# Seven half products for eight in the q, k, gate and v projections of a linear-attention layer

## The chip, the cores and the metric

The kernel runs on one core of a Trainium2 chip. The metric is the device time in microseconds (us) of one execution. TensorE is called PE in the rows of the profile, its weight loads PEld, VectorE DVE, ScalarE ACT, GpSimd POOL, and SyncE SP, whose queue issues transfers.

## The reference

The layer takes 1024 tokens (4 batches of 256) of 512 features. 32 heads of 128 make q, k and v (silu of a projection) and a gate (sigmoid of a projection); a decayed causal attention without softmax, an RMS norm over all heads, the gate and an output projection follow. Then a residual, a layer norm and a small mixture of low-rank experts on a base matrix.

```
qkv = silu(x @ qkv_w.T)                       # 1024 x 512 by 512 x 12288
q, k, v = heads of qkv                        # 32 heads of 128
attn = scan over blocks of 32 tokens: (q k^T * decay) v + (q * decay) kv
xf = attn * rsqrt(mean(attn^2) + eps) * norm_w
x1 = layernorm(x + (sigmoid(x @ gate_w.T) * xf) @ out_w.T)
...
out = layernorm(x1 + x1 @ base_W.T + base_b + routed low-rank experts of x1)
```

## The kernel before

**Numbers.** Every large product is computed in three passes: each operand is split in a high part (a copy to the type fp32r, on ScalarE) and a low part (what is left, a subtraction on VectorE), and TensorE adds high x high, high x low and low x high into one PSUM bank (`mm3`, L736 to L738). So every weight chunk, q, k, v, the masked scores and the gated attention cost one ScalarE copy and one VectorE subtraction (`minus`, L425) beside the matmuls.

**Stages.** The heads run in 8 groups of 4. In a group each head s has a q, a k and a gate projection: 4 slices of 128 features by two halves of 512 tokens, so 2 x 4 x 3 matmuls of 512 columns each for q, k and gate. The values of the four heads come together (8 token tiles x 4 x 3 matmuls of 512 columns). `scores` and `attention` use matmuls of 256 and 128 columns, four batches in a row. The output projection of the group before (8 tiles x 4 heads x 3 matmuls) lies at the head s = 1 of the next group. After the last group come the last output products, the sum of squares, the first layer norm, transposes, router, base product and second layer norm: about the last 70 us.

**Order.** Nothing is scheduled by a tool. Each engine runs its own list in the order of the code and waits on counters (semaphores). PSUM has 8 banks: 0 to 3 are filled in turn by projections, 4 to 7 hold scores, attention and output. A projection may start when the bank that it takes has been read (`bank_free`), that is four projections earlier; each projection bank is read once, by one silu or tanh.

**Loads.** Weights come as 170 chunks of 256 KB into 5 buffers (`raw`) and are split into 10 buffers (`wh`, `wl`). GpSimd does nothing in the groups; it works in the last 70 us, where it adds the residual (L701), the bias (L707) and the statistics of the layer norms (L691 to L694). The squares for the RMS norm are added by VectorE (L481).

## Time and profile before

| | us |
|---|---|
| median of 3 runs | 1094.51 (1093.79 to 1096.12) |
| profiled execution, its own time | 1093.89 |
| its span on the core | 1092.1 |
| PE busy | 1077.2 (99%), 5403 matmuls |
| DVE busy | 664.7 (61%) |
| ACT busy | 533.3 (49%) |
| POOL busy | 47.5 (4%) |

1.8 us of the profiled execution's own time lie outside its span. A matmul's recorded duration is longer than the distance to the next one, because matmuls are pipelined; the distance between starts is what a matmul costs.

### The profile page before, as it was taken

The page shows a single profiled execution, that of the slowest core. Times are in us where ns is not written, and L with a number is a line of the kernel's source. Part 1 is how long each engine was busy: PE and PEld are TensorE (multiplying, and loading weights), DVE is VectorE, ACT ScalarE, POOL GpSimd, SP SyncE. Part 2 cuts the span into 40 slices and gives each one's busy share as a digit, 9 for nine tenths or more (in the row PEclk, how much of TensorE's full clock was granted, in tenths as well). Part 3 has the DMA queues.
Part 4 walks back from the last instruction along what each step waited for, and adds up shares of the span by engine and source line. Part 5 has one row for each costly group of instructions (what it writes and reads, how often), then busy time and mean ns, then how long its engine had stood idle before and what let it go on. Part 6 is the DMA issues. An engine that isn't in the chain of part 4 may idle for free.

```text
span 1092.1 us, 14420 instructions
## 1 busy us (share of the span) xinstructions
PE 1077.2 (99%) x5403; PEld 914.6 (84%) x5403; DVE 664.7 (61%) x1308; ACT 533.3 (49%) x987; POOL 47.5 (4%) x89
## 2 busy tenths in 40 slices
PE   9999999999999999999999999999999999999996
PEld 7888888888888888888888888888888888888784
DVE  6477653774547635676437755486456674477766
ACT  7465541555416543465416555165433654265433
POOL 1000000000000000000000000000000000000365
PEclk9999999999999999999999999999999999999998
DMA  7031111111102102111011111021020110211202
GB/s 258 18 117 34 54 32 41 54 40 49 53 21 79 42 20 73 52 36 53 18 55 54 35 53 54 20 60 62 20 73 33 55 53 5 68 54 34 73 1 78
DMA packets 34055, 56.95 MB, mean 52 GB/s; under 512 B 4416, under 2 KB 8896, under 8 KB 33984
## 3 DMA queue, kind: packets, MB, share of 16 engines
q1 hardware_dynamic: 29088, 51.55, 14.5%
q10 hardware_dynamic: 4896, 4.46, 1.4%
q8 instruction: 43, 0.70, 0.3%
q14 instruction: 28, 0.23, 0.1%
HBM read 53.90 MB, written 2.10 MB: 51 GB/s over the span
## 4 chain that ended last, share of the span: by engine, by line
PE 96%; POOL 1%; DVE 1%; DMA 0%; issue 0%; ACT 0%; SPq 0%; POOLq 0%
PE ps L736 31%; PE ps L738 30%; PE ps L737 30%; PE ps L828 1%; PE ps L807 1%; PE ps L809 1%; PE ps L830 1%; POOL acc L701 0%; DMA acc<-xt 0%; POOL rstd L693 0%; POOL neg_mean L691 0%; PE ps L889 0%; ACT acc L367 0%; POOL var_eps L692 0%; PE ps L899 0%
## 5 line engine op out<-in xcount | busy, mean ns | idle before, releaser
L736 PE MATMUL ps<-xh,wh 128*128 128x512 f32 x764 | 302.4, 396 | 0.0
L738 PE MATMUL ps<-xh,wl 128*128 128x512 f32 x764 | 298.4, 391 | 0.0
L737 PE MATMUL ps<-xl,wh 128*128 128x512 f32 x764 | 297.7, 390 | 0.0
L266 ACT ACTIVATE sig<-ps 128x512 f32<-128x512 f32 x192 | 110.3, 592 | 148.9 <-PE ps L738 133.4
L738 PEld LDWEIGHTS ps<-xh,wl 128*128 128x128 f32 x764 | 143.4, 188 | 31.5
L736 PEld LDWEIGHTS ps<-xh,wh 128*128 128x128 f32 x764 | 143.7, 188 | 28.7 <-DVE wl L425 0.3
L737 PEld LDWEIGHTS ps<-xl,wh 128*128 128x128 f32 x764 | 143.8, 188 | 28.3
L284 ACT ACTIVATE s<-sfull 128x384 fp32r<-128x384 f32 x128 | 67.2, 525 | 117.8 <-DVE sfull L449 117.8
L736 PE MATMUL ps<-wh,xh 128*128 128x512 f32 x288 | 114.0, 396 | 0.3 <-DVE xl L425 0.3
L738 PE MATMUL ps<-wh,xl 128*128 128x512 f32 x288 | 113.0, 392 | 0.0
L737 PE MATMUL ps<-wl,xh 128*128 128x512 f32 x288 | 112.8, 392 | 0.0
L425 DVE TENSOR_TENSOR wl<-raw,wh 128x512 fp32r<-128x512 f32 x170 | 106.9, 687 | 4.0 <-ACT wh L345 3.0
L425 DVE TENSOR_TENSOR vl<-sig,vh 128x512 fp32r<-128x512 f32 x64 | 43.6, 691 | 100.3 <-ACT vh L272 100.3
L736 PE MATMUL ps<-wh,yh 128*128 128x512 f32 x256 | 100.0, 391 | 0.0
L738 PE MATMUL ps<-wh,yl 128*128 128x512 f32 x256 | 99.7, 389 | 0.0
L737 PE MATMUL ps<-wl,yh 128*128 128x512 f32 x256 | 99.7, 389 | 0.0
L292 ACT ACTIVATE sfull<-ps 128x256 f32<-128x256 f32 x64 | 23.4, 380 | 155.4 <-PE ps L830 155.4
L492 DVE TENSOR_TENSOR acc<-acc,ps 128x512 f32<-128x512 f32 x56 | 38.5, 688 | 92.8 <-PE ps L738 92.8
L443 DVE TENSOR_TENSOR sfull<-ps,dec 128x256 f32<-128x256 f32 x128 | 53.7, 420 | 58.7 <-PE ps L809 58.7
L257 ACT ACTIVATE wh<-raw 128x512 fp32r<-128x512 f32 x160 | 88.7, 620 | 1.6 <-DMA raw<-stream 1.6
L425 DVE TENSOR_TENSOR q<-sig,q 128x512 fp32r<-128x512 f32 x64 | 44.3, 693 | 61.7 <-ACT q L272 61.7
L425 DVE TENSOR_TENSOR s<-sfull,s 128x384 fp32r<-128x384 f32 x128 | 71.0, 555 | 7.8
(123 smaller groups left out, 1659.4 us busy)
## 6 DMA issues: line engine op xcount, KB each, us to landing
raw<-stream SPq DMA_DIRECT2D x170, 256.0 KB, 2.9
dec<-decay ACTq DMA_DIRECT2D x34, 128.0 KB, 2.0
acc<-xt SPq DMA_DIRECT2D x8, 256.0 KB, 4.8
raw<-x SPq DMA_DIRECT2D x8, 256.0 KB, 2.6
out<-acc SPq DMA_DIRECT2D x8, 256.0 KB, 2.0
ar<-lora_router SPq DMA_DIRECT2D x1, 288.0 KB, 3.1
sq<-base_b SPq DMA_DIRECT2D x1, 256.0 KB, 3.1
ident<-ident_in SPq DMA_DIRECT2D x1, 64.0 KB, 2.7
```

What stands on the lines that cost most here:

```text
L257: nc.scalar.activation(wh[:, u % AHEAD, :], raw[:, (AHEAD + u) % RAW, :], ACT.Copy)\
L266: nc.scalar.activation(sig[:, n % 2, :], ps[:, PROJ_B + i % 4, :], ACT.Silu).then_inc(silu_full, 1)
L284: nc.scalar.activation(sh[:, b, :], sfull[:, b % 2, 0:SC], ACT.Copy).then_inc(s_hi, 1)
L292: nc.scalar.activation(by_batch(sfull[:, e, 0:SEQ]), att_banks(e, SEQ, SC), ACT.Copy)\
L425: return nc.vector.tensor_tensor(dst, full, f32(hi), ALU.subtract)
L443: nc.vector.tensor_tensor(full[:, SEQ:W].rearrange("p (a n) -> p a n", a=2), part[:, SEQ:W].rearrange("p (a n) -> p a n", a=2), dec[:, s % ...
L492: nc.vector.tensor_tensor(acc[:, t, :], acc[:, t, :], ps[:, AO_B + t % 2, :], ALU.add)\
L736: nc.tensor.matmul(dst, wt[0], mv_[0], start=start, stop=False)
L737: nc.tensor.matmul(dst, wt[0], mv_[1], start=False, stop=False)
L738: return nc.tensor.matmul(dst, wt[1], mv_[0], start=False, stop=stop)
L807: nc.tensor.matmul(ps[:, S_B + b, SEQ:W], kh[:, q0 + P:q0 + SEQ], q2[:, :, q0 + P:q0 + SEQ], start=True, stop=False)
L809: nc.tensor.matmul(ps[:, S_B + b, SEQ:SC], kl[:, q0 + P:q0 + SEQ], qh[:, q0 + P:q0 + SEQ], start=False, stop=True).then_inc(s_done, 1)
```

## The change

The operands of the projections are cut in 2 x 2 halves: features of x in two halves, tokens in two halves, weight columns in two blocks. The product of such matrices is made of 7 half products in place of 8 (Strassen's method in Winograd's form). A block of work is one such product: the two columns blocks are q and k of one head (`qk0` to `qk3`), the gates of two heads (`g01`, `g23`), or two pairs of heads for the values (`V0`, `V1`, by token tiles). A group has the eight blocks QK0, V0, V1, G01, QK1, G23, QK2, QK3.

- The seven token operands (four quarters and three sums) are made once, at the start, on VectorE and GpSimd. Their high and low parts take 7 x 1024 columns each (before 4 x 1024).
- The seven weight operands of a block are four loaded units of 256 columns and three sums, which GpSimd makes in three additions (`sums`). ScalarE copies the high parts in two instructions of 768 and 1024 columns, VectorE subtracts twice.
- Half product p1 goes to bank 0. ScalarE copies bank 0 to bank 1 (`u2_copy`); p6 adds onto bank 1, p2 onto bank 0. ScalarE copies bank 1 to bank 2 (`u3_copy`); p7 adds onto bank 2, p3 onto bank 1. p5 has bank 3 and is copied to SBUF (`p5_copy`). VectorE adds it to bank 2 (`c22_add`) and to bank 1 (`c12_add`). p4 adds onto bank 2 and is issued in the next block, behind its p1. Bank 0, 2 and the two sums are the four results.
- A half product is 6 matmuls of 512 columns for q, k and gates, and 12 of 256 columns for the values.
- The high parts of q and k come from a second silu in place of a copy; the value's split and the splits of y are made per head and per tile, in wider or rearranged instructions.
- `scores` and `attention` are issued in two parts of two batches each.
- The squares are added by GpSimd (`add_squares`), and the next attention part on ScalarE waits for that addition, since both use the buffer `sq`. The head weights `norm_w` are applied to the output weights in place of y.
- The output projection stands behind V1 and uses banks 0 and 3. Loads are blocks of 512 KB into two stage buffers; decay tables are issued by SP in place of ScalarE.

```diff
+UNIT = {1: 0, 5: 1, 6: 2, 2: 3, 7: 4, 3: 5, 4: 6}
...
-            def project(g, i, c, e, ready=None):
-
-                bank_free(g, i)
-                r = c % AHEAD
-                for k in range(KT):
...
-                    last = mm3(ps[:, PROJ_B + i % 4, :], (wh[:, r, tile(k)], wl[:, r, tile(k)]),
-                               (xh[:, k, half(e)], xl[:, k, half(e)]), k == 0, k == KT - 1)
...
+            def features(i, bank, name, start, stop):
+
+                slot = (SLOT[name] + UNIT[i]) % RING
+                for k in range(2):
+                    last = mm3_onto(ps[:, bank, :], (wh[:, slot, tile(k)], wl[:, slot, tile(k)]),
+                                    (xh[:, i - 1, half(k)], xl[:, i - 1, half(k)]), start and k == 0, stop and k == 1)
...
+            def values(i, bank, step, start, stop):
+
+                for t in range(2):
+                    dst = ps[:, bank, t * U:t * U + U]
+                    tok = 2 * step + t
+                    for k, name in enumerate(("va", "vb")):
...
+                        last = mm3_onto(dst, (xh[:, i - 1, xs], xl[:, i - 1, xs]), (wh[:, slot, :], wl[:, slot, :]),
...
+            def p1(n):
...
+                pe.wait_ge(c11_out, n)
...
+            def p4(n):
...
+                pe.wait_ge(c22_added, n + 1)
+                product(4, B2, n, stop=True)
...
+            def with_scores(n, h):
+                p1(n)
+                p4(n - 1)
+                p5(n)
+                scores(h, 0)
+                p6(n)
+                scores(h, 1)
+                p2(n)
+                p7(n)
+                p3(n)
...
+            def sums(g, name):
...
+                nc.gpsimd.tensor_tensor(stage[:, s, 1:5:3, :], stage[:, s, 0:6:5, :],
+                                        stage[:, s, 7:8, :].broadcast_to([P, 2, U]), ALU.add).then_inc(t_part, 1)
...
+                nc.gpsimd.tensor_tensor(stage[:, s, 2, :], stage[:, s, 1, :], stage[:, s, 5, :], ALU.add)\
...
+                nc.gpsimd.tensor_tensor(stage[:, s, 6, :], stage[:, s, 2, :], stage[:, s, 3, :], ALU.add)\
...
+            def u3_copy(n):
+                act.wait_ge(p_done[6], n + 1)
+                act.wait_ge(c21_out, n)
+                act.wait_ge(c22_added, n)
+                copy(ps[:, B2, :], ps[:, B1, :]).then_inc(cp12, 1)
...
+            def part(h, e):
+                act.wait_ge(att_done, 2 * h + e + 1)
+                act.wait_ge(sq_added, 2 * h + e)
+                copy(by_batch(sq[:, 0:SEQ]), att_banks(e, SEQ, SC)).then_inc(att_part, 1)
...
+            def c22_add(n):
+                dve.wait_ge(p_done[7], n + 1)
...
+                nc.vector.tensor_tensor(c22_pre, ps[:, B2, :], p5s, ALU.add).then_inc(c22_added, 1)
```

**VectorE, around one head's scores.** Before, in the middle of a group (`sfull` is the masked score, `s` its split, `wl` a weight's low part, `q` and `kl` low parts of q and k):

```order
L443 TENSOR_TENSOR sfull<-ps,dec 128x256 [waits s_done,s_lo]
L446 TENSOR_TENSOR sfull<-ps,dec 128x256
L449 TENSOR_TENSOR sfull<-sfull 128x128 [waits s_parts]
L425 TENSOR_TENSOR s<-sfull,s 128x384 [waits s_hi] x2
L425 TENSOR_TENSOR wl<-raw,wh 128x512 [waits split_hi] x5
L425 TENSOR_TENSOR q<-sig,q 128x512 [waits silu_hi] x2
L425 TENSOR_TENSOR kl<-sig,kh 128x512 [waits silu_hi] x2
```

After, in block G23 (`stg` holds the two sums; L852 is `c22_add`, L859 `c12_add`):

```order
L819 TENSOR_TENSOR q<-stg,q 128x512 [waits c21_out,q1_full]
L819 TENSOR_TENSOR wl<-stage,wh 128x768 [waits t_hi]
L892 TENSOR_TENSOR sfull<-ps,dec 128x2x256 [waits dec_in1,sc_done,s_lo]
L894 TENSOR_TENSOR sfull<-ps,dec 128x2x256
L898 TENSOR_TENSOR sfull<-sfull 128x2x128 [waits s_parts]
L819 TENSOR_TENSOR s<-sfull,s 128x768 [waits s_hi]
L892 TENSOR_TENSOR sfull<-ps,dec 128x2x256 [waits sc_done,s_lo]
L894 TENSOR_TENSOR sfull<-ps,dec 128x2x256
L898 TENSOR_TENSOR sfull<-sfull 128x2x128 [waits s_parts]
L819 TENSOR_TENSOR wl<-stage,wh 128x1024 [waits t_hi]
L852 TENSOR_TENSOR stg<-ps,stg 128x512 [waits c22_out,k1_lo,cp5,p7_done]
L859 TENSOR_TENSOR stg<-ps,stg 128x512 [waits c12_out,k0_lo,cp5,p3_done]
```

The addition for which p4 of TensorE waits (L852) now stands behind both masks of the head and a weight's low part.

**ScalarE, from one head's q and k to the next copies.** Before:

```order
L266 ACTIVATE sig<-ps 128x512 [waits silu_lo,proj_done] x2
L272 ACTIVATE q<-sig 128x512 [waits silu_full]
L266 ACTIVATE sig<-ps 128x512 [waits silu_lo,proj_done]
L272 ACTIVATE q<-sig 128x512 [waits silu_full]
L266 ACTIVATE sig<-ps 128x512 [waits silu_lo,proj_done]
L272 ACTIVATE kh<-sig 128x512 [waits silu_full] x2
```

After, from the end of block QK1 into G23 (L394 is a silu, L350 a copy; the last row but one is `p5_copy`):

```order
L394 ACTIVATE kh<-stg 128x512 [waits sc_done,c22_added]
L394 ACTIVATE stg<-stg 128x512 [waits k1_hi]
L394 ACTIVATE kh<-stg 128x512 [waits sc_done,c12_added]
L394 ACTIVATE stg<-stg 128x512 [waits k0_hi]
L350 ACTIVATE vh<-v 128x1024 [waits att_done]
L350 ACTIVATE ps<-ps 128x512 [waits c12_added,p1_done]
L394 ACTIVATE stg<-ps 128x512 [waits q0_lo,p4_done]
L394 ACTIVATE q<-ps 128x512 [waits sc_done]
L350 ACTIVATE stg<-ps 128x512 [waits c22_added,c12_added,p5_done]
L350 ACTIVATE wh<-stage 128x768 [waits p4_done,t_sum]
```

The copy from bank 0 to bank 1 (`ps<-ps`) now stands behind the four silus of k and the copy of the values, and what TensorE, VectorE and ScalarE do in a block depends on each other in both directions.

## Rows read from the trace of the kernel before

**Rows 1.** The page: busy time, granted clock by slices, chain of waits.

```profile
PE 1077.2 (99%) x5403; PEld 914.6 (84%) x5403; DVE 664.7 (61%) x1308; ACT 533.3 (49%) x987; POOL 47.5 (4%) x89
...
PEclk9999999999999999999999999999999999999998
...
PE 96%; POOL 1%; DVE 1%; DMA 0%; issue 0%; ACT 0%; SPq 0%; POOLq 0%
```

**Rows 2.** TensorE in order of time (start, us, engine, line, operation), at 299 to 317 us.

```profile
299.74 0.39 PE L736 MATMUL ps<-wh,yh 128*128 128x512 f32 x1
...
314.47 0.39 PE L738 MATMUL ps<-wh,yl 128*128 128x512 f32 x1
314.70 0.28 PE L736 MATMUL ps<-s,vh 128*128 128x256 f32 x1
314.81 0.28 PE L737 MATMUL ps<-s,vh 128*128 128x256 f32 x1
314.93 0.28 PE L738 MATMUL ps<-s,vl 128*128 128x256 f32 x1
...
317.00 0.46 PE L736 MATMUL ps<-xh,wh 128*128 128x512 f32 x1
317.29 0.40 PE L737 MATMUL ps<-xl,wh 128*128 128x512 f32 x1
```

**Rows 3.** Groups of ScalarE and VectorE (count, busy us, mean ns, idle before).

```profile
L266 ACT ACTIVATE sig<-ps 128x512 f32<-128x512 f32 x192 | 110.3, 592 | 148.9 <-PE ps L738 133.4 <-DVE q L425 14.7 <-DVE vl L425 0.8
...
L284 ACT ACTIVATE s<-sfull 128x384 fp32r<-128x384 f32 x128 | 67.2, 525 | 117.8 <-DVE sfull L449 117.8
...
L425 DVE TENSOR_TENSOR wl<-raw,wh 128x512 fp32r<-128x512 f32 x170 | 106.9, 687 | 4.0 <-ACT wh L345 3.0 <-ACT wh L257 1.0
L425 DVE TENSOR_TENSOR s<-sfull,s 128x384 fp32r<-128x384 f32 x128 | 71.0, 555 | 7.8
L443 DVE TENSOR_TENSOR sfull<-ps,dec 128x256 f32<-128x256 f32 x128 | 53.7, 420 | 58.7 <-PE ps L809 58.7
```

**Rows 4.** A projection's last matmul and the ScalarE instruction that reads it.

```profile
343.47 0.39 PE L738 MATMUL ps<-xh,wl 128*128 128x512 f32 x1
...
343.90 0.60 ACT L279 ACTIVATE gate<-ps 128x512 f32<-128x512 f32 x1 [1.12 <-PE ps L738]
```

**Rows 5.** GpSimd's groups, then VectorE and GpSimd in the last 70 us.

```profile
L701 POOL TENSOR_TENSOR acc<-acc,raw 128x512 f32<-128x512 f32 x5 | 6.4, 1283 | 0.8 <-ACT acc L362 0.8
...
L694 POOL TENSOR_TENSOR shift<-neg_mean,rstd 128x1 f32<-128x1 f32 x16 | 3.4, 212 | 1.3
```

**Rows 6.** VectorE and GpSimd in order of time, where both work.

```profile
1030.54 0.73 DVE L565 SCALAR_TENSOR_TENSOR acc<-acc,rms,raw 128x512 f32<-128x512 f32 x1
...
1030.78 0.55 POOL L694 TENSOR_TENSOR shift<-neg_mean,rstd 128x1 f32<-128x1 f32 x1
...
1036.72 0.69 DVE L425 TENSOR_TENSOR xl<-ps,xh 128x512 fp32r<-128x512 f32 x1 [0.61 <-ACT xh L372]
1036.76 1.29 POOL L701 TENSOR_TENSOR acc<-acc,raw 128x512 f32<-128x512 f32 x1
...
1058.33 0.22 DVE L603 TENSOR_TENSOR equal<-prob,top 128x60 f32<-128x60 f32 x1
...
1067.17 5.01 POOL L727 TENSOR_TENSOR acc<-acc,raw 128x512 f32<-128x512 f32 x4 [10.06 <-ACT raw L386]
...
1067.35 1.19 DVE L603 TENSOR_TENSOR equal<-prob,top 128x60 f32<-128x60 f32 x1
```

**Rows 7.** The start: token chunks reaching ScalarE, TensorE's third projection.

```profile
5.53 0.63 ACT L350 ACTIVATE xh<-acc 128x512 fp32r<-128x512 f32 x1 [0.90 <-DMA acc<-xt]
6.51 0.63 ACT L350 ACTIVATE xh<-acc 128x512 fp32r<-128x512 f32 x1 [0.35 <-DMA acc<-xt]
...
12.42 0.50 PE L736 MATMUL ps<-xh,wh 128*128 128x512 f32 x1
```

**Rows 8.** The page: weight loads, issue to landing.

```profile
raw<-stream SPq DMA_DIRECT2D x170, 256.0 KB, 2.9
```

More of the change, by code:

```diff
@@ L23 @@
 W = 512
+U = 256
 SC = SEQ + P
@@ new lines, in after_gates, with qk1 @@
+            def after_gates(n, h, first, second):
+                u2_copy(n)
+                g21_out(n - 1)
+                first()
+                p5_copy(n)
+                part(h, 0)
+                square(h, 0)
+                u3_copy(n)
+                part(h, 1)
+                square(h, 1)
+                q0_out(n, h + 1)
+                second()
+                k1_out(n, h + 1)
+                k0_out(n, h + 1)
+                values_hi(h + 1)
+            def qk1(g):
+                after_gates(NB * g + QK1, HG * g, lambda: sums_hi(g, "g23", "A"), lambda: sums_hi(g, "g23", "B"))
@@ new lines, in _, with product, units_ready @@
+            NAMES = {QK0: "qk0", G01: "g01", QK1: "qk1", G23: "g23", QK2: "qk2", QK3: "qk3"}
+            def product(i, bank, n, start=False, stop=False):
+                b = n % NB
+                if b in (V0, V1):
+                    last = values(i, bank, b - V0, start, stop)
+                else:
+                    last = features(i, bank, NAMES[b], start, stop)
+                last.then_inc(p_done[i], 1)
+            def units_ready(n, part):
+                b = n % NB
+                name = "vb" if b in (V0, V1) else NAMES[b]
+                pe.wait_ge(t_lo, 2 * load_no(n // NB, name) + (1 if part == "A" else 2))
@@ L870, in _ @@
[L870 to L875 removed]
+                    last = nc.tensor.matmul(ps[:, S_B + b, SEQ:SC], kl[:, q0 + P:q0 + SEQ], qh[:, q0 + P:q0 + SEQ],
+                                            start=False, stop=True)
+                last.then_inc(sc_done, 1)
@@ new lines, in _ @@
+            pe.wait_ge(zeros_set, 1)
+            zero = s2[:, 0, :, :].rearrange("p b n -> p (b n)")
+            for i in range(WARMUP):
+                nc.tensor.matmul(ps[:, B1 + i % 2, :], zero[:, 0:P], zero[:, 0:W], start=True, stop=True,
+                                 skip_group_check=True)
+            for g in range(GROUPS):
+                n, h = NB * g, HG * g
+                qk0(g)
+                v0(g)
+                v1(g)
+                if g > 0:
+                    output(g)
+                g01(g)
+                with_attention(n + QK1, h)
+                with_scores(n + G23, h + 1)
+                with_attention(n + QK2, h + 1)
+                with_scores(n + QK3, h + 2)
```

1554 lines of the change are left out of this document (1101 added, 453 removed).

## The prediction

> **What bounds the kernel now.** I read the page first: PE is busy for 99% of the span at full granted clock (the slices show 9 in all but the last), and the chain of waits is 96% PE [rows 1]. The kernel is bound by the number of matmul columns. Then TensorE in order of time, for what a matmul costs: from 299.74 to 314.47 us lie 65 starts of 512-column matmuls, 14.73 / 65 = 0.2266 us each. 256-column matmuls start 0.11 to 0.12 us apart; I take 0.118. The section of four batches takes 317.00 - 314.70 = 2.30 us, and the matmul behind it is late by 0.06 (0.29 where 0.2266 is usual), together about 0.1 us for entering and leaving a section of short matmuls [rows 2]. The other engines have room: ACT 49%, DVE 61%, POOL 4% [rows 1]. ScalarE's silu waited 133 us in total for TensorE, and VectorE's masks 59 us [rows 3]: they wait for PE, hardly ever PE for them.
>
> **What TensorE saves.** q, k and gates had 32 x 3 x 2 x 4 x 3 = 2304 matmuls of 512 columns; 7/8 of them is 2016. 288 x 0.2266 = 65.3 us less. The values had 768 matmuls of 512 columns (174.0 us) and get 8 x 2 x 84 = 1344 of 256 columns (1344 x 0.118 = 158.6 us): 15.5 us less. Scores and attention go in 128 parts of two batches in place of 64 of four: 64 more sections at 0.1 = 6.4 us more. Net: -74.4 us. Output, tail and base matmuls keep their number. If nothing else cost anything: 1093.9 - 74.4 = 1019.5.
>
> The Trainium skill, "TensorE: Matmul & The Clock Gate", section "Back-to-back issue gap", speaks against cutting the values' matmuls in two: it gives a sustained 81 ns for 128 columns and 131 ns for 512, so that a half is far more than half a price. By the mean of its two figures, an estimate of 106 ns against 131, the values would cost 42 us more instead of less. This trace differs on both figures (227 and 118 ns) [rows 2], and I go by the trace.
>
> **What the change puts on the others.** Per group of 4 heads TensorE then needs (1019.5 - 90) / 8, about 118 us. ScalarE: 8 blocks x (three bank copies at 0.6, weights 0.85 + 1.05) = 29.6; silus of q and k 16 x 0.6 = 19.2 (each of k's two waits for the other); values and gates 16 outputs, 9.6; splits of values, scores, y 16; attention parts and squares 8; output weights 3: some 86 us, 73%. VectorE, by 555 and 687 ns for 384 and 512 columns, hence 0.95 for 768 and 1.21 for 1024 [rows 3]: weights 17.3, the two additions of each block 11, q and k low parts 11, masks 14.4, other splits 18, the rest 17.5: about 89 us, 76%. GpSimd, by 1283 ns for 512 columns and 212 for one, 2.1 ns a column [rows 5]: three additions of 512, 256, 256 columns are 2.8 us a block, and eight squares 10.3: 32.7 us a group, 28%. No sum reaches 118. What matters is that each list is in order and that the lists now wait for each other in both directions.
>
> **Where the lists miss each other.** The handover from PE is 343.90 - (343.47 + 0.227) = 0.20 us [rows 4]; 0.05 between ACT and DVE and 0.15 back to PE (wait plus a weight load) are my estimates, below that row. Half products take 1.36 us. ScalarE's 768 and 1024 columns are taken as 0.85 and 1.05, between 0.72 and 1.05 for the first by half or twice the slope of its rows. I walk through block G23; t = 0 is its p1.
> - ScalarE leaves QK1 with a backlog from p2 on: two silus of q, weights part B, two silus of k1, two of k0 (k0 waits for `c12_add`, p3 being the last half product), values. It ends at about 3.9. Then `u2_copy` 4.5, q1 5.6, `p5_copy` 6.1, weights A 7.0, `u3_copy` 7.5. These still meet p6 and p7.
> - VectorE: low part of A until 7.8, mask 9.5. ScalarE: scores 10.4, weights B 11.3, and g11 (the output of bank 0) 11.9, while the next p1 needs it at 12.0. VectorE goes on: scores' low part, second mask 13.0, low part of B 14.1, and only then `c22_add` 14.8. The next p4 should start at 13.3: 1.6 us late.
> - In the same way: start of QK0 0.7, its p4 1.1 (the same place in QK3's list), its scores 0.55 (they wait for attention part, square and gate of the head before, behind two weight copies), V0's p4 1.0 and p6 0.95 (`u2_copy` stands behind k0's silus), V1 0.4; in QK3 0.5.
> Sum: 2.1 x 8 + 4.7 x 7 = 49.7 us.
>
> **Once each.** Start: before, the third projection begins at 12.42 us, when 24 matmuls (5.4 us of work) are done, so TensorE runs 7.0 us behind a start at zero [rows 7]; QK0's 42 matmuls, 9.5 us, would end at 16.5. Now VectorE has 19 instructions of up to 1024 columns between the first token quarter (6.5 us: four chunks are there then) and the first low parts of the values' weights: about 18.6 us less overlaps, so V0 starts at 25.2: +8.7. Group 0 has no output products to cover the weights of G01, whose buffers come free with V1's last product: silu, scores, values, A, low part: +5.0. The end: head 31's chain of split, scores, mask, attention, square has fewer products beside it: 1.1 + 2.7 + 1.6 + 1.1 + 2.8 + 1.4 = +10.7. Sum 24.4 (between 10, if half is hidden by tail products, and 35).
>
> **GpSimd and VectorE exclude each other.** This is what decides. At 1058.33 VectorE compares 60 columns in 0.22 us; at 1067.35 the same instruction takes 1.19, until GpSimd's first addition (1067.17, 1.25 each) is over. The other way, GpSimd's one-column product of 0.21 took 0.55 at 1030.78, until VectorE's instruction ended at 1031.27. But at 1036.72 a subtraction that has one operand in PSUM took its usual 0.69 beside a GpSimd addition [rows 6]. So an instruction of VectorE with both inputs in SBUF waits for GpSimd's running one, and the reverse. The Trainium skill, "SBUF — State Buffer", section "SBUF: two separate sides", calls it an exclusive lock for the whole instruction; the trace agrees. Of VectorE's 89 us in a group 53 are such instructions (all low parts, the masks' last addition), against 32.7 us of GpSimd. If the lock hit evenly, a GpSimd addition would find VectorE wanting it in half its time: 32.7 x 53/118 = 14.7 us of waiting a group, shared by both. With GpSimd's additions put in where their loads land (2.9 us for 256 KB [rows 8], 4 taken for a block), the walk above changes: in G23 A's low part waits 0.7, the mask's addition until 10.3, so g11 comes at 13.1: p1 of QK2 1.15 late and p4 1.55; QK2 0.3, QK3 0.85, start of QK0 1.75, its p4 1.1, its scores 2.1, V0 2.3, V1 0.4. Sum 3.85 x 8 + 7.65 x 7 = 84.4. The start gets 6 more (x sums and weight sums of GpSimd beside low parts), G01 0.4, the end 3: 33.8.
>
> **The sum:** 1093.9 - 74.4 + 84.4 + 33.8 = 1137.7; the median of the runs is 0.6 above the profiled execution. I say **1137**, with 1112 to 1168 for this case (one third of the group's waits away, or a quarter more with once-only costs at 35). Chance 0.50.
>
> **The rivals.**
> - *GpSimd works beside VectorE's gaps.* The lock costs its time where VectorE waits anyway (it has 24% of slack): 1093.9 - 74.4 + 49.7 + 24.4 = 1093.6, between 1075 and 1105. For it: GpSimd is idle 72% of the time. Against: the additions start when a load lands, in the middle of a block, which is where the masks are. Chance 0.22, half of it faster.
> - *The lists keep up* (the other side). The waits of a few tenths to 1.6 us exist only if ScalarE and VectorE take what the means say; two instructions in a row overlap, and if the backlog behind k0's silus is 1.5 us shorter, nearly all group waits go: what is left is the once-only part: 1093.9 - 74.4 + 20 = 1040, with 1025 to 1065. It decides by `c22_add` ending before p1 of the next block does. Chance 0.19.
> - *VectorE saturates.* Its 36 us of other work and 53 + 32.7 of the lock one behind the other are 122 us a group, over TensorE's 118; with in-order waits 140: 1190. Chance 0.09. It would need GpSimd's additions to be hit by most low parts.
> - The change does what it says: the 2016 and 1344 matmuls can be counted in the program; no chance is set aside.
>
> **How the numbers follow.** Faster by over 0.2% (about what a measurement of this kernel can tell from no change): 0.19 + 0.11 + 0.01 = 0.31; within 0.2% 0.04; slower 0.65. The range leaves out half of the rival that keeps up and most of the saturated one: 1045 to 1168; the likeliest case's own range is 1112 to 1168.
>
> **What would show it.** PE busy falls below 95%; the wait list of PE names `stg` (`c22_add`), `ps<-ps` and g11's silu or tanh; DVE rows of 768 columns with a mean well over 0.95, at times 1.7 or more; GpSimd's 512-column additions over 1.28; V0 starting later than 25 us. I am wrong if PE waits less than 3 us a group, if VectorE's means stay at 0.95 and 1.21, or if 256-column matmuls of the values start over 0.13 us apart.

## The result, and the profile after

The changed kernel takes 1175.65 us (median of 4 runs, 1171.3 to 1178.05), the kernel before 1094.29 (4 runs, 1093.79 to 1096.12): ratio 1.074, 95% interval 1.070 to 1.077. It is slower, as forecast, but by 81 us where the forecast said 43; the time lies 8 us above the range. The profiled execution took 1174.22 us, its span is 1172.3.

The page of the changed kernel, the rows that answer to [rows 1] (busy time, slices of TensorE and of its granted clock, chain):

```profile
PE 1047.5 (89%) x5690; PEld 889.9 (76%) x5690; DVE 788.6 (67%) x1095; ACT 665.1 (57%) x1092; POOL 363.3 (31%) x347
...
PE   5889898999899898988899998998989988998896
...
PEclk8889999999899998999989999999989999999998
```

TensorE is busy for 30 us less and the span is 80 us longer. The new thing beside the gaps is in the clock row: the first three slices are 8, and an 8 comes back four times in the middle of the kernel, where [rows 1] has nines up to the last slice.

TensorE's waits in the changed kernel (what it waited for: us in total, times, the longest):

```profile
PE ps L1414 <- DVE yl L819: 26.2, 7, 4.1
PE ps L1420 <- DVE stg L852: 25.7, 23, 1.8
PE ps L1420 <- DVE wl L819: 15.4, 3, 5.7
PE ps L1414 <- DVE y L919: 11.0, 8, 1.8
PE ps L1414 <- DVE wl L838: 7.7, 6, 1.4
PE ps L1420 <- ACT q L394: 7.1, 8, 1.1
PE ps L1420 <- ACT ps L350: 5.0, 8, 0.8
```

`stg` at L852 is `c22_add`, `y` at L919 the gate on the attention, `yl` at L819 the low part of y for an output tile, `wl` at L838 an output weight. The first row, the largest, and the row of `wl` at L838 belong to the output stage and have no counterpart in the prediction.

**Where the time went.** I sorted the distance between each matmul's start and the next into four heaps: what the columns cost at full clock (0.2267 us for 512, 0.118 for 256, 0.19, 0.11 and 0.06 for 384, 144 and 128); distances that the trace marks with a wait; distances of 0.36 to 0.6 us behind a 512-column matmul and of 0.19 to 0.3 behind a 256-column one without a wait, which are matmuls at half speed (only what they cost over full speed counts); the rest (entering short sections, the first matmul behind a wait, merged rows, start of the span). Each column is one profiled execution.

| us of the span | before | changed | difference | in the sum |
|---|---|---|---|---|
| columns at full clock | 1043.4 | 963.5 | -79.9 | -80.8 |
| waits | 6.2 | 126.8 | +120.6 | +118.2 |
| half speed | 1.8 | 26.8 | +25.0 | 0 |
| rest | 40.7 | 55.2 | +14.5 | +6.4 |
| span | 1092.1 | 1172.3 | +80.2 | +43.8 |

So the sum missed 25 us in a term it did not have, 8 in the rest, 2.4 in the waits and 1 in the columns.

**Where half speed stands.** Taking each half-speed matmul to the last wait before it, the trace of the changed kernel gives: behind the seven waits of 3.7 to 4.1 us in the output stage 13.5 us of the 26.8 (behind six of the seven); at the start, at G01 of group 0 and in the last 75 us most of the rest. Between 60 us and the last 75 us lie 66 waits of under 1.5 us, 56.8 us in all, and behind them stand 3.1 us. So it was the long waits that cost clock, and the longest of each group is the one that the prediction did not have.

**One wait from near.** The output stage of group 3 in the changed kernel, VectorE and GpSimd, then TensorE (start, us, engine, line, operation):

```profile
440.40 2.69 DVE L838 SCALAR_TENSOR_TENSOR wl<-stage,nw,wh 128x512 fp32r<-128x512 f32 x2
443.00 1.22 DVE L819 TENSOR_TENSOR yl<-y,yh 128x512 fp32r<-128x512 f32 x1
444.14 0.68 DVE L892 TENSOR_TENSOR sfull<-ps,dec 128x512 f32<-128x512 f32 x1
...
446.79 0.96 DVE L819 TENSOR_TENSOR s<-sfull,s 128x768 fp32r<-128x768 f32 x1 [0.91 <-ACT s L350]
447.74 2.21 DVE L819 TENSOR_TENSOR vl<-v,vh 128x1024 fp32r<-128x1024 f32 x1
449.88 0.67 DVE L932 TENSOR_TENSOR acc<-acc,ps 128x512 f32<-128x512 f32 x1
450.48 0.68 DVE L819 TENSOR_TENSOR yl<-y,yh 128x512 fp32r<-128x512 f32 x1
```

```profile
440.11 1.30 POOL L1335 TENSOR_TENSOR stage<-stage 128x512 f32<-128x512 f32 x1 [7.92 <-DMA stage<-stream]
441.49 1.05 POOL L1338 TENSOR_TENSOR stage<-stage 128x256 f32<-128x256 f32 x1
442.61 1.06 POOL L1342 TENSOR_TENSOR stage<-stage 128x256 f32<-128x256 f32 x1
446.88 2.00 POOL L1335 TENSOR_TENSOR stage<-stage 128x512 f32<-128x512 f32 x1 [3.21 <-DMA stage<-stream]
```

```profile
451.21 0.79 PE L1414 MATMUL ps<-wh,yh 128*128 128x512 f32 x1 [3.69 <-DVE yl L819]
451.81 0.63 PE L1415 MATMUL ps<-wl,yh 128*128 128x512 f32 x1
452.23 0.63 PE L1416 MATMUL ps<-wh,yl 128*128 128x512 f32 x1
```

All three causes are here. The low part wanted at 447.5 stands on VectorE behind a mask, scores' and values' low parts that nothing wants for many microseconds (order). Two 512-column instructions of L838 take 2.69 us, where the same line has a mean of 0.75 for one in the run without GpSimd reads below, and the 1024 columns 2.21 where they have 1.22 there: GpSimd's sums run beside them (exclusion). And the matmuls behind the wait start 0.42 us apart, not 0.2266 [rows 2]: half speed. The stretches of the same kernel show it as granted clock (columns: stretch, length, PE, PEld, DVE, ACT and POOL busy, PEclk, DMA share, GB/s):

```profile
440.00:446.00 6.00, 4.62 (x22) 3.51 (x21) 5.84 (x7) 2.24 (x6) 3.41 (x3) 1.00 0.27 71
451.50:456.00 4.50, 4.50 (x11) 3.51 (x11) 3.39 (x4) 0.00 (x0) 0.24 (x1) 0.50 0.03 5
457.00:462.00 5.00, 5.00 (x24) 4.10 (x23) 2.63 (x4) 1.06 (x2) 3.10 (x3) 1.00 0.19 64
```

1.00 is 2.4 GHz and 0.50 is 1.2 GHz. What the engine did before it fell: a wait of 3.7 us.

### The profile page after: what moved, and what is told of

Same layout as the page of the kernel before. It is cut to its first block and busy times, and to the rows that moved or that the text cites. A ratio compares the mean times of both kernels' runs of the same rounds, so it can differ in the third digit from the quotient of the medians.

```text
span 1172.3 us, 15829 instructions
## 1 busy us (share of the span) xinstructions
PE 1047.5 (89%) x5690; PEld 889.9 (76%) x5690; DVE 788.6 (67%) x1095; ACT 665.1 (57%) x1092; POOL 363.3 (31%) x347
## 5 line engine op out<-in xcount | busy, mean ns | idle before, releaser
L1420 PE MATMUL ps<-xh,wh 128*128 128x512 f32 x672 | 274.8, 409 | 49.7 <-DVE stg L852 25.7
L1335 POOL TENSOR_TENSOR stage<-stage 128x512 f32<-128x512 f32 x64 | 99.1, 1549 | 502.5 <-DMA stage<-stream 502.5
L819 DVE TENSOR_TENSOR wl<-stage,wh 128x768 fp32r<-128x768 f32 (+3 forms) x149 | 161.2, 1093 | 73.6 <-ACT wh L350 73.6
L1355 POOL TENSOR_TENSOR sqacc<-sqacc,sq 128x512 f32<-128x512 f32 x64 | 82.6, 1290 | 260.8 <-ACT sq L491 260.8
L350 ACT ACTIVATE wh<-stage 128x768 fp32r<-128x768 f32 (+3 forms) x149 | 124.8, 853 | 37.3 <-PE ps L1416 33.7
L1420 PE MATMUL ps<-wh,xh 128*128 128x256 f32 x448 | 130.9, 292 | 9.3 <-DVE wl L819 5.1
L1414 PE MATMUL ps<-wh,yh 128*128 128x512 f32 x232 | 98.2, 423 | 34.0 <-DVE yl L819 26.2
L1422 PE MATMUL ps<-wh,xl 128*128 128x256 f32 x448 | 127.1, 284 | 0.0
L1421 PE MATMUL ps<-wl,xh 128*128 128x256 f32 x448 | 127.0, 284 | 0.0
L350 ACT ACTIVATE s<-sfull 128x768 fp32r<-128x768 f32 x64 | 54.1, 846 | 123.7 <-DVE sfull L898 123.7
L1420 PEld LDWEIGHTS ps<-wh,xh 128*128 128x128 f32 x448 | 85.9, 192 | 11.9 <-ACT ps L350 5.6
L350 ACT ACTIVATE ps<-ps 128x512 f32<-128x512 f32 x128 | 74.7, 584 | 27.5 <-PE ps L1422 26.7
L1421 PEld LDWEIGHTS ps<-wl,xh 128*128 128x128 f32 x448 | 86.4, 193 | 0.4
L1422 PEld LDWEIGHTS ps<-wh,xl 128*128 128x128 f32 x448 | 86.1, 192 | 0.0
L819 DVE TENSOR_TENSOR s<-sfull,s 128x768 fp32r<-128x768 f32 x64 | 61.8, 966 | 35.1 <-ACT s L350 35.1
```

The costliest lines, as they stand in the source:

```text
L350: return nc.scalar.activation(dst, src, ACT.Copy, **kw)
L819: return nc.vector.tensor_tensor(dst, full, f32(hi), ALU.subtract)
L1335: nc.gpsimd.tensor_tensor(stage[:, s, 1:5:3, :], stage[:, s, 0:6:5, :], stage[:, s, 7:8, :].broadcast_to([P, 2, U]), ALU.add).then_inc(t_p ...
L1355: nc.gpsimd.tensor_tensor(sqacc[:, e, :], sqacc[:, e, :], sq[:, :], ALU.add).then_inc(sq_added, 1)
L1414: nc.tensor.matmul(dst, wt[0], mv_[0], start=start, stop=False)
L1420: nc.tensor.matmul(dst, wt[0], mv_[0], start=start, stop=False, skip_group_check=True)
```

## The experiments

My theories: **A**, exclusion of VectorE and GpSimd makes the waits; **B**, the order of the in-order lists does; **C**, a wait also costs clock. The times are medians of four or more timed runs; the kernel before gave 1093.8 to 1094.2 beside each.

### GpSimd without operands: two runs and a control

```
-  nc.gpsimd.tensor_tensor(stage[...], stage[...], stage[...], ALU.add)    # three a load
+  nc.gpsimd.memset(region, 0.01)                                          # six a load, chained
```

> The changed kernel, but GpSimd's three additions of each weight load (three tensor additions, two inputs each) are replaced by six memsets of the same regions, chained in the same way; the weight sums are left out, all matmuls, splits and waits stay. A memset reads nothing from SBUF. Theory A (the waits of TensorE come from VectorE and GpSimd excluding each other, as the prediction had it): the waits of the groups fall from about 15 us a group towards 8 and the time by most of the 26 us that the prediction put on this (84.4 less 49.7, and 33.8 less 24.4, less what the squares still cost): 1140 to 1155 us. Theory B (the order of VectorE's and ScalarE's lists makes the waits, the exclusion only lengthens some): the time falls by less than 15 us, 1160 to 1175. Theory C (a long wait of TensorE lowers its clock, which then costs as much again): if the wait in the output stage stays (3.7 us), the half-speed stretches behind it stay too.

> As the run before it, and the two additions of squares of each head on GpSimd are also replaced by two memsets each, so that GpSimd reads no SBUF operand beside VectorE in any group; weight sums and sums of squares are left out. Theory A: 44 us less than the changed kernel (34.7 of the groups, 9.4 of start and end), 1130 us, and VectorE's splits of 768 columns back from a mean of 1193 to about 966 ns. Theory B: 1155 to 1175 us, and the waits at the output stage and ahead of the scores remain in size and place. Theory C: the time falls by more than the waits do, since half-speed stretches go as well.

(in the second run also `sqacc` two memsets for each addition of squares)

Both kernels leave out the sums, so they don't compute the layer; they are for their time alone. Measured: 1124.2 us, 51.5 less; with the squares too 1111.7, 63.9 less. Far more than either theory had said. Waits fell to 85.3 and 77.4 us, and in the page of the second VectorE's busy time to 739.8 us from 788.6. But the chain of memsets was shorter than the additions. The control has nine, as long as the additions:

```
+  regions = [stage 1,4] * 3 + [stage 2] * 3 + [stage 6] * 3
```

> The first memset kernel had two differences from the changed kernel at once: GpSimd read nothing beside VectorE, and its chain for a load was shorter (six memsets, about 2.3 us by the rows of that run, against about 3.6 us), so that the splits of weights could start 1.3 us earlier. Here the chain is as long as the additions: nine memsets, three of 512 columns at 526 ns and six of 256 at 312 ns, 3.45 us. Weight sums are left out as before. If exclusion between VectorE and GpSimd is what costs, the time stays at 1124 us (within 5 us). If it was the earlier end of the sums, it returns to 1165 us or more. Half and half: 1145 us.

Measured: 1135.0 us, 40.7 less, between the case of exclusion alone (1124) and half and half (1145). So some four fifths of the first run's gain are exclusion, 11 us were the earlier end of the sums. VectorE's splits of 768 columns, in the changed kernel and in the control (count, busy us, mean ns, idle before):

```profile
L819 DVE TENSOR_TENSOR wl<-stage,wh 128x768 fp32r<-128x768 f32 x55 | 65.6, 1193 | 49.0 <-ACT wh L350 49.0
```

```profile
L819 DVE TENSOR_TENSOR wl<-stage,wh 128x768 fp32r<-128x768 f32 x55 | 52.6, 957 | 49.0 <-ACT wh L350 49.0
```

The idle time ahead of them is the same, only the duration changed: beside a memset VectorE's split is not held. The Trainium skill, "SBUF — State Buffer", section "SBUF: two separate sides", limits the lock for VectorE's two-input operations to a GpSimd operation that reads SBUF; these two rows agree. TensorE's waits in the control show what exclusion was worth at each place:

```profile
PE ps L1420 <- DVE stg L852: 25.0, 23, 1.8
PE ps L1414 <- DVE yl L819: 15.2, 7, 2.2
PE ps L1414 <- DVE y L919: 3.2, 8, 1.6
```

In the output stage the wait goes from 3.7 us to 2.2 and those for L838 are gone; `c22_add` is as late as before (25.7 to 25.0). So the waits for `c22_add`, and 2.2 of the 3.7 us, are left when the exclusion by the sums is gone.

### The same contention in the kernel before

GpSimd, idle there, makes eight times a group four products of 512, 256, 256 and 512 columns that nobody waits for.

```
+  pool.wait_ge(proj_done, g * NPROJ + 4 * i + 1)
+  for cols in (512, 256, 256, 512):
+      nc.gpsimd.tensor_tensor(ar[0:cols], ar[0:cols], ones, ALU.mult)
```

> The kernel before the change, with GpSimd set to work that no engine waits for: eight times a group four element-wise operations with two SBUF operands (512, 256, 256, 512 columns, about 4 us together), the amount of the changed kernel's weight sums and squares. Shows the exclusion alone, in the lists of the kernel before, where VectorE is 69% busy too. If the exclusion costs whatever the lists are (it lengthens VectorE's splits and TensorE waits for them): 1110 to 1150 us. If it costs only where the lists leave no slack: 1094 to 1098 us, with VectorE's splits longer in the trace and nothing waiting for them.

Measured: 1094.3 us, ratio 0.9999 (0.9989 to 1.0008). In its trace the splits of [rows 3] take 814 ns where they took 687, and VectorE is busy 60.7 us longer than [rows 1] has it:

```profile
L427 DVE TENSOR_TENSOR wl<-raw,wh 128x512 fp32r<-128x512 f32 x170 | 128.9, 814 | 3.2 <-ACT wh L346 3.2
```

```profile
PE 1078.5 (99%) x5403; PEld 915.4 (84%) x5403; DVE 725.4 (66%) x1308; ACT 531.6 (49%) x987; POOL 307.2 (28%) x346
```

(VectorE is busy for 61% in the kernel before [rows 1], not for the 69% of the expectation.) This is the run that decides what "exclusion costs" means. GpSimd is busy for 28% against 31% in the changed kernel, VectorE's splits are longer, and TensorE doesn't notice: its waits are 5.9 us by the heaps, for 6.2. That the lists of before have the wanted things early is my reading of it. Exclusion by itself costs no time; it is paid through a list without slack.

### What a wait costs by itself

In the kernel before, TensorE waits ahead of an output tile for a chain on GpSimd (of one-column powers) that began when an earlier tile was done.

```
+  if t in tiles: pe.wait_ge(stall, ...)     # tiles = [2], chain of 12; or [2, 4, 6], chains of 8
```

> The kernel before the change, with one artificial wait of TensorE in the output stage of groups 1 to 7: ahead of token tile 2 it waits for a chain of 12 power operations on one column on GpSimd (568 ns each in the trace of before, 6.8 us and more), which starts when tile 0 is done, 2.7 us earlier. Nothing else changes. A wait of about 4.1 to 4.6 us seven times, 29 to 32 us by itself. If a wait costs only its length: 1123 to 1127 us. If TensorE's clock falls to half behind a wait of this length, as behind the waits of the changed kernel (2.3 us of extra per stretch there): 1140 us or more, with stretches of granted clock near 0.5 behind each.

> The kernel before the change, with three artificial waits per group in place of the one: ahead of token tiles 2, 4 and 6 TensorE waits for a chain of 8 power operations of GpSimd (4.5 us and more) that starts 2.7 us earlier, so 1.8 to 2.2 us each, 21 times, 38 to 46 us in all. If a wait costs only its length: 1132 to 1140 us. If short waits too lower the clock, there are 21 half-speed stretches and 1165 us or more; if only a wait as long as 3.7 us does, none, and 1132 to 1140 us.

The waits made, one long a group and three short ones:

```profile
PE ps L744 <- POOL var_eps L720: 36.5, 7, 5.3
```

```profile
PE ps L744 <- POOL var_eps L720: 55.5, 21, 2.7
```

The waits came out longer than planned, 5.2 us in place of 4.1 to 4.6 and 2.65 in place of 1.8 to 2.2, so waits of 2 us were not tried in this kernel. Measured: 1149.4 us, 55.3 more for 36.5 us of waits; 1179.0, 84.9 more for 55.5. By the same heaps half-speed matmuls cost 16.6 and 22.5 us more than in the kernel before, 2.4 behind a wait of 5.2 us and 1.1 in the mean behind one of 2.65 (1.4 to 1.7 behind 15 of the 21, nothing behind the other six, which are the first wait of a group in groups 2 to 7). Theory C holds for waits of these lengths: in the middle of dense matmuls they cost 1.5 times their length. It does not hold for every wait. The 66 waits of under 1.5 us in the changed kernel had 3.1 us of half speed behind them, and among longer ones the share with a half-speed stretch behind them grows: of 2.0 to 2.2 us 8 of 14 (in the second memset run and in the first reorder below), of 2.65 us 15 of 21, of 3.7 to 4.1 us six of seven in the changed kernel, of 5.2 us seven of seven. The stretches around one of the short waits, with the columns of the stretches above (the wait is in the first, the second lies behind it):

```profile
458.00:463.00 5.00, 2.46 (x11) 1.69 (x9) 1.15 (x2) 0.00 (x0) 4.34 (x9) 1.00 0.00 0
463.70:466.80 3.10, 3.10 (x9) 2.42 (x8) 0.00 (x0) 0.00 (x0) 0.00 (x0) 0.50 0.00 0
```

### One place reordered: two misses

```
 VectorE, blocks G23 and QK3
-  scores_lo(h, 0); mask(h, 1); sums_lo(B); c22_add; c12_add; scores_lo(h, 1)
+  scores_lo(h, 0); c22_add; mask(h, 1); c12_add; sums_lo(B); scores_lo(h, 1)
```

> The changed kernel with one reorder of VectorE's list: in the sections of the second gate pair (G23) and of QK3 the two PSUM additions stand ahead of the second half mask and of the low parts of the next weights. Result unchanged. TensorE's fourth products wait 0.9 to 1.4 us for the first of these additions 23 times, 25.7 us in all. Theory A (exclusion) and theory B (list order) differ in size: if the order of the list is what makes this wait, two of three of them go, about 2.4 us a group or 16 to 19 us in all, 1157 to 1160 us, unless the mask that now stands behind comes late for the second scores (then the wait moves there and the time is within 5 us of 1175). If exclusion makes it, no more than 8 us.

```
 VectorE, output stage
-  mask(h, 1); scores_lo(h, 1); values_lo(h); out_add(0); y_low(2); sums_lo(A); out_add(1); y_low(3)
+  out_add(0); y_low(2); out_add(1); y_low(3); mask(h, 1); scores_lo(h, 1); values_lo(h); sums_lo(A)
```

> The changed kernel with one reorder at the output stage: ScalarE copies the high parts of y of token tiles 2 and 3, and VectorE adds output tiles 0 and 1 and makes the low parts of tiles 2 and 3, ahead of the second mask and of the high and low parts of the values (these are only wanted 20 us later). Result unchanged. The wait of TensorE ahead of tile 2 (3.69 to 4.1 us, 7 times, 26.2 us in all) should go. Theory B with a clock that stands for itself: 1149 us (26 us less). Theory C (TensorE's clock falls to half behind this wait, which doubles its cost): the half-speed stretches that follow it go too, 2.3 us or more each, 1130 to 1135 us. Theory A (exclusion by GpSimd's sums, which run in the same stretch): the wait moves to the next VectorE operation wanted, 1165 to 1175 us.

Measured: 1171.0 and 1178.7 us. Both edits did what they said at their place, and the wait turned up elsewhere. In the first the waits for `c22_add` fell from 25.7 to 6.9 us, but those for q's silu rose from 7.1 to 16.1. All waits together were 9.1 us less, but half-speed matmuls cost 35.1 us in place of 26.8, since seven of these waits are now of 2 us, and five of the seven have 1.6 to 1.9 us of half speed behind them. Its trace at one of the seven, ScalarE, GpSimd and TensorE:

```profile
513.85 0.38 ACT L350 ACTIVATE sq<-ps 128x256 f32<-128x256 f32 x1 [3.86 <-POOL sqacc L1355]
...
515.71 0.60 ACT L394 ACTIVATE q<-ps 128x512 fp32r<-128x512 f32 x1
```

```profile
509.58 1.29 POOL L1335 TENSOR_TENSOR stage<-stage 128x512 f32<-128x512 f32 x1 [10.11 <-DMA stage<-stream]
510.95 0.74 POOL L1338 TENSOR_TENSOR stage<-stage 128x256 f32<-128x256 f32 x1
511.77 0.74 POOL L1342 TENSOR_TENSOR stage<-stage 128x256 f32<-128x256 f32 x1
512.47 1.29 POOL L1355 TENSOR_TENSOR sqacc<-sqacc,sq 128x512 f32<-128x512 f32 x1
```

```profile
516.45 0.47 PE L1420 MATMUL ps<-xh,wh 128*128 128x512 f32 x1 [2.04 <-ACT q L394]
```

Before the change the squares were added by VectorE. Now the addition stands on GpSimd behind weight sums that wait for their load, ScalarE needs the one buffer `sq` back, and q's silu stands behind that. In the second run the block of other work, kept whole, moved the wait of 4 us from tile 2 to tile 4 (29.5 us in all for 26.2).

### The lists reordered in earnest

Interleaved output stage: between two pairs `out_add(t - 2); y_low(t)` stands one other piece, not four.

```
 VectorE, ScalarE alike
+  out_add(0); y_low(2); out_add(1); y_low(3); mask(h, 1); out_add(2); y_low(4); scores_lo(h, 1);
+  out_add(3); y_low(5); values_lo(h); out_add(4); y_low(6); sums_lo(A); out_add(5); y_low(7); ...
```

> The changed kernel with the output stage interleaved: on VectorE each addition of an output tile and the low part of y for the tile two behind it stand together, and one other piece (second mask, scores' low part, values' low part, G01's weights A, B) stands between two such pairs; ScalarE's high parts alike. Result unchanged. In the earlier reorder the whole bundle of other work stood as one block and the wait of 4 us only moved from tile 2 to tile 4. Here no block is longer than 2 us against the 2.7 us of a tile. If the order of the lists makes this wait, 26 us of waits go, and by the runs with artificial waits (a wait of 5.2 us cost 7.9 in all, one of 2.6 us 4.0) about half as much again: 1175 less 36 to 40, 1136 to 1140 us. If exclusion by GpSimd's sums in this stretch makes it, less than 15 us: above 1160.

Measured: 1136.1 us, as theory B with C's price had it. The waits are 25.7 us less, half speed went from 26.8 to 16.0 us, and the clock row has no 8 left between start and tail: 39.6 us for a wait of 26.2.

Middle blocks, the first edit above with what its trace showed:

```
 GpSimd    -  next_sums("qk0"); add_squares(h + 1, 0)     +  add_squares(h + 1, 0); next_sums("qk0")
 GpSimd    +  wait for the output weights' low parts, ahead of sums("g01")
 ScalarE   -  sums_hi(B); g11_out / q0_out                +  g11_out / q0_out; sums_hi(B)
```

> The changed kernel with the second addition order (the two PSUM additions ahead of the second mask in G23 and QK3) and with what the first such run showed to stand behind it: on GpSimd the first addition of squares of QK2's head goes ahead of the sums for the next QK0, because ScalarE waited 3.9 us for it (the sums had waited for their load), the output of bank 0 goes ahead of the second part of weights on ScalarE in G23 and QK3, and the sums for G01 wait until the output weights' low parts are done. Result unchanged. If the queue behind a DMA on GpSimd is what kept the first such run from its gain: the waits for the PSUM addition and for bank 0 fall from 33 to under 12 us, and with half as much again 1140 to 1150 us. If not, above 1160.

Measured: 1139.5 us, at the edge of what was expected. Here the waits (heap of the table) fell by 33.5 us and half speed did not fall (31.8 us): the output stage's waits of 3.5 us were all still there, and the waits that went had been short ones. Both, with QK0's attention part, square and gate ahead of the weight splits:

```
 VectorE, QK0
-  sums_lo("va", "B"); q1_low; add_part; gated; sums_lo("vb", "A"); add_part; gated; values_lo; mask
+  q1_low; sums_lo("va", "A"); add_part; gated; sums_lo("va", "B"); add_part; gated; sums_lo("vb", "A"); mask
 ScalarE, end of QK0
-  k0_out; u2_copy                               +  u2_copy; k0_out
```

> Both of the above, and in QK0 the attention part, square and gate of the head before stand ahead of the weight splits, the values' splits behind the outputs, and V0's copy between banks ahead of k's silus. Result unchanged; GpSimd's work is all there. If orders and exclusion together are the whole of it, an order in which no urgent instruction stands behind a splittable one leaves mostly start and end: waits of about 45 us in place of 127, 1075 to 1095 us. If VectorE's exclusion cannot be hidden by order, 1110 to 1130 us, as much as the run without any exclusion at best.

Measured: 1105.2 us, ratio 1.0105 (1.0088 to 1.0121), between the two cases expected. The two gave 39.6 and 36.1 alone, 75.7 if added, and 70.4 together with QK0's edit: they add up in the main, and what QK0's edit gave can't be told from this. TensorE's waits are down to 69.2 us. All of GpSimd's work is still there, and the time is already below that of the run without any of it. The last two versions went after what the trace still listed.

```
 ScalarE   -  k0_out; sums_hi("va", "A"); u2_copy      +  u2_copy; k0_out; sums_hi("va", "A")
 ScalarE   -  square; v11_out                          +  v11_out; square
 GpSimd    -  sums("vb"); add_squares(h - 2, 0)        +  add_squares(h - 2, 0); sums("vb")
 group 0   -  SLOT g01 13, qk1 4, g23 11, qk2 2, qk3 9 +  5, 12, 3, 10, 1
 start     -  nc.gpsimd.tensor_tensor(x and va, vb sums)  +  nc.vector.tensor_tensor(...)
```

> The last reordered kernel (1105 us) and five more edits, result unchanged: (1) QK0's first copy between banks ahead of k's silus, and the square's addition of the head before ahead of the sums for the values on GpSimd (waits of 1.1, 0.2, 1.5 and 0.6 us in QK0 of every group); (2) the output of bank 0 ahead of the square in V0 (0.8); (3) in group 0 the weights of G01 to QK3 lie in other slots of the ring, so that G01's weights need not wait for V1's last half product (4.5 once); (4) at the start the sums of tokens and of the values' weights are made by VectorE, one by one, instead of GpSimd beside it, and both parts of the first weights ahead of them (4.5 and 4.3 once); (5) at the end head 28 and 29's splits and the last masks ahead of weight rows (3.0, 1.5 and 2.5 once). If the waits of TensorE and their clock are the whole of what the change costs: 4.1 x 7 + 0.8 x 7 less a rest of 1.5 x 7 is 24, start and end 10 to 14, clock 4: 1063 to 1075 us, below the kernel before for the first time. If a wait taken away here comes back at the next product: 1085 to 1105.

Measured: 1096.8 us, ratio 1.0023 (1.0013 to 1.0033). 8 us of about 35 aimed at, as the second case had it. In QK0 of each group 1.6 us came back ahead of the first scores and 1.2 at V0: the bank copy had gone ahead, but the attention part now stood behind q's silus and a weight copy.

```
 ScalarE   end of QK3:  u2_copy; part(h, 0); k0_out; square(h, 0)     (part and square came in QK0)
 VectorE   QK0:         gated; mask; c22_add; sums_lo("vb", "A")      (the weights came first)
 start:    values' weights ahead of c22_add, a token split and c12_add
```

> The last kernel (1096.8 us) with the waits that its trace still shows in QK0 of every group attacked: ahead of the first scores 1.6 us (the attention part of the head before stood behind q's output and a weight copy on ScalarE), V0's first half product 1.25 (values' weights behind a wait for GpSimd's second addition of squares), V0's fourth 0.6. Now the attention part and the square stand ahead of k's silus, and VectorE's mask and PSUM addition ahead of the values' weights. At the start the values' weights go ahead of two PSUM additions and a token split (4.7 once), in group 0 the bank copy of G01 ahead of the values' high part (3.0 once). Result unchanged. If waits that come from the order of the lists are all that is left: 3.4 x 7 + 4, and little clock: 1068 to 1076 us. If VectorE is simply full in QK0, so that each gain there is lost again at the next product (as 1105 to 1097 may mean, where 24 us of waits had been aimed at in the groups and 7 came): 1088 to 1097.

> The same with GpSimd's additions of groups replaced by memsets that read nothing and last as long (weight sums of the groups and sums of squares are left out; group 0's first sums stay on VectorE). What is left of the exclusion once the order is good. In the changed kernel it was 40 us with the squares still there. If a good order hides it: within 8 us of the run before it. If the exclusion costs as much as before whatever the order: 40 us or more below it.

Measured: 1081.5 us, ratio 0.9885 (0.9869 to 0.9902): 12.6 us below the kernel before. The same without exclusion: 1057.8, 23.7 less. Both lie between the two cases that had been expected: the gains do not all come back at the next product, and order hides a part of the exclusion, not all. The page of the first:

```profile
PE 1026.5 (95%) x5690; PEld 886.9 (82%) x5690; DVE 764.9 (71%) x1104; ACT 660.3 (61%) x1093; POOL 343.2 (32%) x339
...
PEclk7999999999999999999999999999999999998998
```

| us of the span | changed | output spread | all lists | last |
|---|---|---|---|---|
| waits | 126.8 | 101.1 | 69.2 | 45.7 |
| half speed | 26.8 | 16.0 | 18.1 | 19.5 |
| span | 1172.3 | 1135.6 | 1102.6 | 1079.2 |

Exclusion was worth 63.9 us in the changed kernel with a shorter GpSimd chain (of which some 11 was that chain) and 23.7 with the last lists. So order hides more than half of it, and the rest is still paid (group 0's first sums are VectorE's in the last lists and not in the second figure): what is left in each group is mostly one wait ahead of V0, for values' weights (3.4 us in group 1, 1.7 in each of groups 2 to 7), whose sums GpSimd makes beside VectorE (last version, group 3):

```profile
499.53 0.39 PE L1489 MATMUL ps<-wh,xh 128*128 128x256 f32 x1 [1.74 <-DVE wl L854]
```

In the run without exclusion GpSimd's group additions, squares too, are memsets as in the control.

## Why the prediction was right and wrong

- **Saving.** Columns: -80.8 foretold, -79.9 measured. The 256-column matmuls of the values start 0.118 to 0.12 us apart, so halving them paid, as the trace of before had it. Short sections: 6.4 foretold, nothing found outside the waits: matmuls at a change of column count cost 14.8 us over the heap's prices before and 14.5 in the changed kernel, and going from 512 to 256 columns cost next to nothing (86 times, -0.1 us). The 14.5 us of the rest are something else: 6.4 the first matmul behind a wait, which is about 0.1 us late in 62 places and so belongs to the waits; 3.3 merged rows, mostly at the start; about 5 ordinary matmuls a little above the heap's prices. The Trainium skill's figures that the prediction weighed ("TensorE: Matmul & The Clock Gate", "Back-to-back issue gap"), by which the values would have cost 42 us more, did not hold here: 512-column matmuls start 0.227 us apart and 256-column ones 0.118 to 0.12, about half.
- **Group waits.** 84.4 us with exclusion, 49.7 without, and once-only 33.8 and 24.4: added, 118.2 and 74.1 against 120.6 and 71.2 measured (in the run without exclusion). As totals these are the best numbers of the prediction; as a list of places they are partly wrong. In group 3, foretold to found: start of QK0 1.75 to 0.81, its p4 1.1 to 0.88, scores 2.1 to 1.83, V0 2.3 to 1.57 (its p4 and p6), V1 0.4 to 0, p1 of QK2 1.15 to 0.20, its p4 1.55 to 1.38, and the start of QK3 0.85 to 1.14. **The output stage was not walked through at all** and has 1.38 and 3.69, the largest of them. The places visited sum to 11.2 foretold and 7.8 found in this group. The walk overrated most of them, which paid for the one it left out: that the sums agree is luck, and no proof of their terms.
- **GpSimd and VectorE exclude each other.** "This is what decides", the prediction says. Half right: the price (44 us in the sum) was, if anything, low; 40.7 for the weight sums alone, and some 12 for the squares (1124.2 less 1111.7). But the run on the kernel before has VectorE busy 60.7 us longer by exclusion, at no cost. It decides only together with the order of the lists, and the reordered lists (with the start's sums given to VectorE and other ring slots in group 0) took 94 us away where taking exclusion away took 64.
- **The failed step: what follows a wait.** The sum added up waits as if TensorE went on at full speed behind them. [Rows 1] had a sign of it: the clock row falls to 8 only in its last slice, in the stretch where TensorE has its longest waits. Term of the sum: 0, measured 25.0. It hangs together with the other gap, the output stage that was not walked through (put at 0, found 26.2 and 7.7 us): 13.5 of the 25.0 us stand behind its waits of 3.7 to 4.1 us. The waits that the walk did have, 0.3 to 2.3 us each, would hardly have called for such a term. So the factor of 1.5 can't be laid on all waits: on the foretold 118.2 us it gives 1197 us, 21 too many. With the 25 measured the forecast would have been 1162.
- **Start and end.** Foretold V0's start at about 31 us, found 33.0; G01 of group 0 5.4, found 4.5; the end 13.7, found 7.8 over five waits. So the once-only places too were overrated, but for V0.
- **Rivals.** "GpSimd works beside VectorE's gaps" (1093.6) had the mechanism for 1111.7 us of the run without exclusion; what it lacks is again clock (19) and the rest. "The lists keep up" (1040) named `c22_add` ahead of p1 as the point that decides; one such edit alone moved the wait elsewhere. "VectorE saturates" (1190) is 14 us away in time but not in mechanism: VectorE is busy for 67%, and the same work in another order takes 94 us less.
- **Signs and slips.** Every sign that the prediction named for its case appeared (PE busy 89%, the wait list, 1193 ns for 768 columns, 1549 ns on GpSimd, V0 at 33 us); none of them could have shown the missing terms. Its bounds don't follow from its words: a third of 84.4 us away gives about 1110, a quarter more with 35 once gives about 1160, and it had 1112 and 1168. A group's need of TensorE, (1019.5 - 90) / 8, is 116 us, not 118; nothing hangs on that.

Not settled: how the 94 us of the reorders divide among their single edits, since all but the first three were run in bundles. Half-speed times are of single executions: the mean granted clock of the four executions of the spread version lay between 0.979 and 0.990 and of the ten of the sixth version between 0.980 and 0.988, so that 20.5 us in the one and 16.0 in the other need no reason of their own. Why some waits of one length have half speed behind them and others have none is open, and no run separates waits near one another from waits far apart. No run moved the loads: GpSimd's sums start when a load lands, and what a third stage buffer would give is open.

## What to carry to other kernels

Price a new wait of TensorE inside dense matmuls at one and a half times its length when it is as long as those tried here (2.65 us and up); the waits of under 1.5 us here cost hardly more than their length. Walk through every stage of a group, the one that the change does not touch as well: new work in a neighbour's list moves there. When a saving on the bound engine is eaten by waits, list for each wait which instruction stood ahead of the late one and when that one's result is wanted; reorder whole chains through all engines (here GpSimd's queue behind a DMA, then ScalarE, then VectorE), since a single swap moves the wait on. Work given to GpSimd with SBUF operands is free only as far as VectorE's list has slack at that moment, whatever the averages of both are.

## What the hardware showed that I had not expected

- A wait of 2.65 us was enough, 15 times of 21, for over 3 us of matmuls at 1.2 GHz behind it (0.43 us apart for 512 columns in place of 0.2267), one of 5.2 us, 7 times of 7, for 2.6 to 6 us. Waits of under 1.5 us had next to nothing behind them.
- VectorE's two-input SBUF instruction beside a GpSimd memset takes its usual time (957 ns for 768 columns); with GpSimd additions in their place its mean is 1193. A GpSimd memset of 512 columns took 526 ns and of 256 columns 312, an addition of 512 columns 1283 undisturbed and 1549 in the mean of the changed kernel.
- At the start of the changed kernel a subtraction of 1024 columns took 1.22 us on VectorE and 3.2 on GpSimd (about 1 us of it waiting for VectorE's running instruction), and VectorE's split of 512 columns, begun beside the first of them, took 2.84 us. In the version that gave these sums back to VectorE V0 began at 30.4 us in place of 32.4, but with other edits of the start in the same bundle.
